# A mixture tile's expert weights: one plain transfer of the sync engine in place of a GpSimd gather

## The reference, cut to what matters

```python
aff = x @ centroids.T                      # 2048 x 8
assign = argmax(aff, axis=1)
xn = xhat[None] * ln_g[:, None] + ln_b[:, None]
h = relu(einsum('etd,efd->etf', xn, w1) + b1[:, None])     # f = 512
y = x[None] + einsum('etf,edf->etd', h, w2) + b2[:, None]
a = sigmoid(aff).T[:, :, None]
gated = a * y + (1.0 - a) * x[None]
out = einsum('te,etd->td', one_hot(assign, 8), gated)
```

```python
probs = softmax(xf @ Ws.T + bs, axis=-1)
routes = argmax(probs, axis=-1)
xf = xf * max(probs, axis=-1)[:, None]
h = relu(einsum('td,edf->etf', xs, W1) + b1[:, None, :])   # f = 128; xs: xf sorted by expert
y = einsum('etf,efd->etd', h, W2) + b2[:, None, :]
out = y[rs, arange(2048)]   # each token's own expert, in the sorted order
```

## Time and profile before

| | us |
|---|---|
| median of 3 runs | 3073.17 (3071.92 to 3073.41) |
| the profiled execution | 3071.25 |
| its span | 3069.2 |
| `l0f_`, from the first weights' gather to the last `ytab` scatter's start | 314.76 to 424.57 |
| `l3f_`, the same | 2963.77 to 3055.53 |

### The profile page before, as it was taken

The page is one execution under the profiler, slowest core; times in us unless marked ns, Lnnn a source line. Parts: engine busy times, 40 slices in busy tenths (PEclk is TensorE's granted clock), DMA queues, the critical chain, the costliest instruction groups (busy, mean ns, idle before and its releaser), DMA issues. The chain is left out here.

```text
span 3069.2 us, 119760 instructions
## 1 busy us (share of the span) xinstructions
PE 2473.0 (81%) x51995; PEld 1899.9 (62%) x51995; DVE 2050.5 (67%) x4945; ACT 1378.3 (45%) x3266; POOL 985.8 (32%) x1200
## 2 busy tenths in 40 slices
PE   8888478999976788888878887659998996788735
PEld 7755365555655676777767676548786664576623
DVE  3447336777749988889788888247777666555741
ACT  5443133444452444444454443347786553554310
POOL 0000434656531533344333444211111440460025
PEclk9879778999987899989898998869999998897855
DMA  3200331111110000000000000002221003241013
GB/s 99 62 1 28 112 111 52 46 45 46 52 53 4 4 4 4 4 4 4 4 4 4 4 4 4 3 20 62 60 62 60 3 4 105 75 99 59 5 59 100
DMA packets 79147, 118.07 MB, mean 38 GB/s; under 512 B 11360, under 2 KB 64240, under 8 KB 78096
## 3 DMA queue, kind: packets, MB, share of 16 engines
q1 hardware_dynamic: 66992, 88.80, 9.2%
q0 software_dynamic: 11696, 22.40, 2.9%
HBM read 98.51 MB, written 16.51 MB: 37 GB/s over the span
## 5 line engine op out<-in xcount | busy, mean ns | idle before, releaser
L3174 PE MATMUL psum<-l1d_rw,l1d_cols 64*32 64x32 f32 (+2 forms) x20480 | 242.0, 214 | 107.4 <-issue 88.5
L3174 PEld LDWEIGHTS psum<-l1d_rw,l1d_cols 64*32 64x32 f32 x20480 | 209.7, 107 | 150.8 <-issue 127.9
L2469 POOL TENSOR_SCALAR l1xs_p<-l1xs_p,l1xs_col 128x257 f32<-128x257 f32 x256 | 233.8, 932 | 204.3 <-DVE l1xs_col L2425 204.3
L2894 POOL TENSOR_TENSOR l1d_tmp<-l1d_lt,l1d_xi 128x64 f32<-128x64 f32 (+1 forms) x96 | 41.7, 462 | 653.7 <-DVE l1d_xi L3525 652.5
L2390 ACT ACTIVATE l1xs_p<-psum,l1xs_col 128x257 f32<-128x257 f32 x256 | 119.6, 473 | 209.2 <-DVE l1xs_col L2420 203.0
L3432 DVE TENSOR_TENSOR l1d_rw<-l1d_rw,l1d_tots 128x1536 f32<-128x1536 f32 x96 | 156.1, 1626 | 55.0 <-PE psum L3174 54.6
L2432 DVE STREAM_TRANSPOSE l1xs_pt<-l1xs_p 128x288 f32<-128x288 f32 x256 | 122.4, 478 | 78.7 <-POOL l1xs_p L2469 78.6
L3111 PE MATMUL psum<-l1d_src,l1d_wp 128*128 128x128 f32 x1024 | 143.3, 298 | 4.3 <-issue 3.0
L3111 PEld LDWEIGHTS psum<-l1d_src,l1d_wp 128*128 128x128 f32 x1024 | 132.8, 210 | 9.0 <-issue 5.3
L2342 PE MATMUL psum<-l1xs_keys,l1xs_qx 128*32 128x257 f32 x2048 | 134.1, 395 | 3.5 <-DVE l1xs_qx L2414 1.9
L2354 PE MATMUL psum<-l1xs_pt,l1xs_vals 32*128 32x512 f32 x1152 | 136.6, 604 | 0.0
(11 more groups left out here) (560 smaller groups left out, 6911.1 us busy)
## 6 DMA issues: line engine op xcount, KB each, us to landing
l2f_w<-in_l2f_w SPq DMA_DIRECT2D x16, 768.0 KB
l1xs_vals<-in_ctx_strips SPq DMA_DIRECT2D x16, 576.0 KB
l0x_ctxT<-in_ctxT SPq DMA_DIRECT2D x16, 516.0 KB, 3.7
l1xs_keys<-in_ctxT SPq DMA_DIRECT2D x16, 516.0 KB
l2x_ctxK<-in_ctxT SPq DMA_DIRECT2D x64, 129.0 KB, 2.1
l2x_ctxV<-in_ctxT SPq DMA_DIRECT2D x64, 129.0 KB, 2.1
l1d_wp<-in_l1d_wp SPq DMA_DIRECT2D x1, 2048.0 KB, 8.3
l2f_acc<-l2f_zero SPq DMA_DIRECT2D x8, 256.0 KB, 3.6
```

The costliest lines, as they stand in the source:

```text
L2469: nc.gpsimd.tensor_scalar(p[:, t % 4, :S2], p[:, t % 4, :S2], col[:, 2, t % 4:t % 4 + 1], None, ALU.mult).then_inc(s["norm"], 1)
L3174: mm = nc.tensor.matmul(k.ps[bank0 + pr + e // per * 2][b * T:b * T + T, e % per * w:(e % per + 1) * w], cols[rr, 2 * n, e * 128 + b * T:e ...
```

## The change

SP transfers a tile's weights. It reads the first row, `w_i[0, j]`, from SBUF into a register (`value_load`) and issues a plain DMA of the 128 rows from there, with the register in its address. The first three tiles' transfers go as soon as `w_i` is there, ahead of the wait for the scatters. The others come behind the five loads of the tiles, each behind the waits for `down` and `results` of the tile that had its slot. POOL keeps the 16 and the 30 scatters in each block. The weights' semaphores, slots and sizes are the same.

```diff
@@ block.sync
         def _(sp):
             norm.sync(sp)
+            def weights(j):
+                if j >= nw:
+                    sp.wait_ge(s["y_mm"], j - nw + 1)
+                    sp.wait_ge(s["y"], halves * (j - nw + 1))
+                first = sp.value_load(w_i[0:1, j:j + 1], min_val=0, max_val=(e - 1) * 128)
+                sp.dma_start(w[:, j % nw, :], k.arr[nm + "w"][bass.ds(first, 128), :]).then_inc(w_in[j % nw], 16)
+
+            sp.wait_ge(s["w_idx"], 1)
+            for j in range(nw):
+                weights(j)
             sp.wait_ge(sent, 16 * NT)
             for n, (j0, j1) in enumerate(groups):
                 sp.dma_start(xin[:, j0:j1].rearrange("p j h c -> p (j h) c"),
                              xtab[j0 * cap:j1 * cap, :].rearrange("(h p) c -> p h c", p=128)).then_inc(x_in[n], 16)
+            for j in range(nw, tiles):
+                weights(j)
@@ block.gpsimd
-            def weights(j):
-                if j >= nw:
-                    pool.wait_ge(s["y_mm"], j - nw + 1)
-                    pool.wait_ge(s["y"], halves * (j - nw + 1))
-                nc.gpsimd.indirect_dma_start(w[:, j % nw, :], None, k.arr[nm + "w"],
-                                             bass.IndirectOffsetOnAxis(ap=w_i[:, j:j + 1], axis=0)).then_inc(w_in[j % nw], 16)
-
-            pool.wait_ge(s["w_idx"], 1)
-            weights(0)
-            weights(1)
             pool.wait_ge(s["place"], 1)
             ...
-            weights(2)
             for j in range(tiles):
                 ...
-                if j + nw < tiles:
-                    weights(j + nw)
```

## The result

| | before | with the change |
|---|---|---|
| median of the runs, us | 3072.55 (3064.16 to 3073.41, 4 runs) | 3039.98 (3031.30 to 3041.78, 4 runs) |
| the profiled execution | 3071.25 | 3031.30 |
| its span | 3069.2 | 3029.5 |

The ratio is 0.9903, with a 95% interval from 0.9876 to 0.9931: faster, and faster than the range of 3046 to 3066 us. The two profiled executions differ by 39.95 us, more than the medians do (32.57).

What follows compares the result with a forecast made beforehand. POOL's indirect DMAs were taken to bound the `l3f_` tiles, TensorE and ACT those of `l0f_`, token scatters the starts. 1.27 + 1.25 + 1.5 + 13.2 + 0.2 = 17.4 us gained, forecasting 3055.8 us, range 3046 to 3066.

Steps and rivals of the forecast that it cites:

- What bounds each stretch before: POOL bounds the `l3f_` tiles, TensorE and ACT those of `l0f_`, 16 token scatters and the load behind them the starts.
- Start of `l0f_`: Token scatters on POOL begin earlier without gathers ahead; one slot gained, 1.27 us (bounds 0.6 and 2.5).
- The load behind the scatters: In `l0f_`, TensorE starts sooner after SP's issue without tile 2's gather between; 1.25 us gained (bounds 0 and 1.25).
- Tiles of `l0f_`: Earlier weights gain 1.5 of the 2.62 us over the 4.71 us rhythm; 1.15 us left as it is.
- Tiles of `l3f_`: POOL's work falls from 3.83 to 2.54 us per tile, TensorE bounds at 2.70; 46.3 instead of 59.53 us, 13.2 gained.
- dry stretches: Two times in `l3f_` when POOL runs dry, 7.2 us, kept in the sum; rival that they go, chance 0.20, 3047.4 us.
- Start of `l3f_`: The first token scatter waited for its row, not for the gathers; 0.2 us gained (bounds 0 and 1.3).
- v: SP's register load with address arithmetic, part of each tile's weight latency; put at 1.05 us, upper bound 2.1.
- One queue for both: In `l3f_`, SP's weights follow the tiles' big loads; up to 2 us latency for tile 3, nothing counted.
- The sum: Gains of both blocks' starts, load and tiles: 1.27 + 1.25 + 1.5 + 13.2 + 0.2 = 17.4 us.
- How the numbers follow: Forecast (0.60) spans 3051 to 3062; 8-in-10 range 3046 to 3066 us; 0.2% (6.1 us) counts as no change.
- The rival that v makes it slower: Chance 0.06: SP's register load with address costs more than 4 us; at 5 us some 10 us slower, 3083.

Runs made afterwards that it cites:

- e3: The changed kernel, with POOL issuing an indirect gather of 128 rows of 520 bytes, read by nobody, in place of each former weights' gather; 3055.78 us, ratio 0.9980.
- f4: The kernel before, with POOL's gather of tile j+3 issued ahead of the two scatters of tile j; 3070.15 us, ratio 0.9993.
- e1: The change in `l0f_` only, while `l3f_` keeps the gathers, against the kernel before; 3053.37 us, ratio 0.9983.
- h1: The changed kernel with each register load ahead of the two waits for the slot instead of behind them; 3035.20 us, ratio 0.9921 to the kernel before.
- f2: The changed kernel with nine register loads in place of one ahead of each transfer; 3096.53 us, ratio 1.0071 to the kernel before.
- e2: The change in `l3f_` only, while `l0f_` keeps the gathers, against the kernel before; 3047.86 us, ratio 0.9954.

## Why the prediction was off, point by point

- **What bounds each stretch before** was right: POOL's slots in the tiles of `l3f_` (e3), TensorE and ACT in those of `l0f_` (the 4.71 us stayed; no run changed these engines' work) with late weights on top (e3, f4), the token scatters ahead of them.
- **Start of `l0f_`**, 1.27 us forecast: right in the first pair. One slot, the fourth scatter held by DVE's sum, last token scatter 1.24 us nearer to the block's start.
- **The load behind the scatters**, 1.25: 1.54 us, and e3 shows that it is the gather's bytes.
- **Tiles of `l0f_`**, 1.5: 2.58 us. I had left 1.15 us aside as a late start of DVE's own; it went too. In e1 and e3 the tiles took 67.2 us as well.
- **Tiles of `l3f_`**, 13.2: this is the term that was mis-sized. It measured 17.7 us in the first pair, and 15 to 17 in pairs from one chip (53.3 to 38.6, 59.1 to 42.3). The step that failed was "TensorE is the slowest, 2.70": I took its pace from two tiles at the 1.2 GHz level and carried that clock over the whole stretch. The pace was right where that clock is granted, 2.69 us in the trace after; but over the stretch the granted clock is 0.74 instead of 0.56, and at 2.4 GHz a tile takes TensorE 1.77 us. So POOL's 29 slots of 1.26 us, the bound in the text and not the value, are 36.6 of the 41.8 us (14 x 2.70 + 1.27 = 39.1 in my sum), and what is left over them is 5.2 us, 2.9 of it a dry stretch, where I had 7.2 us of dry stretches. That is 2.5 and 2.0 of the 4.5 us that the term missed.
- **Start of `l3f_`**, 0.2: 0.1 us at the first scatter and 0.3 more up to TensorE.
- **v**, 1.05 us: 0.82 in `l0f_`, 0.8 to 4.4 in `l3f_` of the first pair and most often 0.8 elsewhere. Single delays over the 2.1 us that the text names as a sign of failure cost little there: TensorE waited 1.3 us for weights. Shortening it gains nothing (h1), and as a pace of SP it decides at 5.2 us (f2). By the Trainium skill (DMA: Bandwidth & Descriptors, "Latency and other measured facts") the load's floor is about 0.6 us; the trace's own row for a load is 0.27 us, the whole sequence up to the issue 0.8, and in f2 one load follows the other by 0.55, so the page's figure is near that last one.
- **One queue for both** was worth counting as nothing: tile 3 did not wait for its weights, and tiles 4 and 5 waited 1.3 us, in which POOL kept its 0.30 us gaps.
- **The sum** of the two blocks was 17.4 us; the first pair has 23.5 there (5.55 + 17.96). By this alone 3072.55 would have become 3049, inside the range. The other 9 us of the median's 32.6 can't be placed, since only one run of each side has a profile; in the profiled pair 17.9 us lie in `l1d_`, which the change doesn't touch. **How the numbers follow** failed here: I took three runs that agreed within 1.5 us as the measure of this kernel, where single executions on one chip spread by 16 to 28 us and chips differ by 19. The range held only doubts about the mechanism and none about the measurement. In the two repeats the change is worth 20.8 and 21.8 us, close to the 18 that e1 and e2 find for the two blocks one by one. Of one kernel against the other that is nearer to the forecast 17.4 than to the measured 32.6; how far the first measurement lies below the forecast is in good part the chance of its four runs.
- **The rival that v makes it slower** is real, but its price was too low and its mechanism another. For 5 us it had `l3f_` 2 us and `l0f_` 8 us longer than before, some 10 us in all; f2, at 5.2 us, has them 15.9 and 10.2 us longer (75.0 against 59.1, 80.0 against 69.8) and is 21.7 us slower, by SP's own pace. Its argument against itself, that every round trip to a memory in the trace is shorter than 4 us, was wrong too: 512 KB took 4.4 us.

## What to carry to other kernels

Where an engine issues every indirect DMA, count its slots per tile first: 1.27 us each bound `l3f_`, and 66 KB in place of 198 KB behind each gather changed little (e3, 52.3 against 53.3 us in e1); and rows that follow one another need only the first one's address, so no indirect DMA at all. When a change quickens the tiles, don't carry TensorE's clock of the slow stretch into the new one: work out its pace at both levels and see on which side of the next bound each falls. And look at the spread of single executions over several chips before a range is drawn around three runs.

## What the runs showed of the hardware

- A register load from SBUF on SP takes 0.27 us; load, assertion and address arithmetic up to the transfer's issue take 0.8 us (`after`), and each further load 0.55 us (f2: nine in 5.2 us). In `l3f_` of `after` single ones took up to 4.4 us.
- A self attention with the same instructions took between 1106.5 and 1125.0 us from execution to execution; in the pair of the first measurement matmuls were busy 18.4 us less with the granted clock at 0.91 for 0.90.
- An indirect DMA of 128 rows mostly holds POOL for 1.26 to 1.29 us, with the 0.30 us to the next one in it, whether a row has 512, 520, 1548 or 4632 bytes. The one that ran beside DVE's long sum took 2.66 to 3.28 us by itself instead of 0.96.
- With the same `l3f_` tiles TensorE was granted 0.53 to 0.57 where POOL had 42 slots and 0.74 to 0.91 where it had 30; in f2, with 30 slots but SP's pace, 0.54.
